# Moving the maximum's products ahead of the first weighing in each turn of an attention kernel on one core

## The chip, the cores and the metric

The kernel runs on one core of one Trainium2 chip. The core has TensorE (PE in the profile, with its weight loads listed apart as PEld), VectorE (DVE), ScalarE (ACT), GpSimd (POOL) and SyncE (SP). Each runs its own stream of instructions in order and waits for the others by semaphores. The metric is the device time of one execution in microseconds (us).

## What is computed

For each of 4 images (512 channels, 48 x 48 = 2304 positions) the layer is group norm, then attention with 8 heads of 64 channels over all 2304 positions, a 1x1 convolution beside it, and the residual. Cut to what matters:

```
h   = groupnorm(x)
q, k, v = (Wq @ h), (Wk @ h), (Wv @ h)          # per head: 64 x 2304
attn = softmax(q^T k)                           # per head: 2304 x 2304
out  = attn @ v
x    = x + gamma * out + Wsc @ h
```

## The kernel before

**Tiling.** Two heads are worked on together (a block; 4 images x 4 pairs = 16 blocks). Head 0 of the pair lies in rows 0 to 63 of TensorE, head 1 in rows 64 to 127, and products of the two halves come in pairs that run beside each other. A block has 6 chunks of 384 queries, so there are 96 chunks (n = 0 to 95). A chunk has 18 turns (k = 0 to 17), one for each 128 keys: 1728 turns, numbered s = 18 n + k.

**One turn on TensorE.** Precision is gained by splitting numbers into an upper and a lower part, so most things are done in several products.
- `score(n, k)`: six products of 384 columns (L477) into the tensor `SL`. It waits until ScalarE has read the scores of the turn before out of `SL` (semaphore `s_exp`).
- `top(U)`, U = s + 22: two products of 384 columns (L451) into `MX`, from which VectorE takes the largest score of each query (L794, one reduction for each `top`). This runs 22 turns ahead, since the maximum of a chunk must be known before its first score. There is one `MX`, so `top(U)` waits until the reduction of `top(U - 1)` has ended (semaphore `s_mxf`). The last 22 turns have no `top`.
- `weigh(s, part)`: the exponentials of turn s times the values, into `OB`. It has two parts, and each is six products of 129 columns (L516) and six of 65 columns (L513). The second part of turn s - 4 is done in turn s, and the first part of turn s - 3.
- `thirds(J, lo, hi)`: projections for the blocks to come (queries, keys, values, or the convolution), into `PJ`, cut into pieces of 128 columns that are spread over the turns: 9, 9, 5 and 13 pieces in turns 0 to 3, mostly 8 or 9 in the others. They are on L386 (384, 256 or 128 columns) or, for values, L384 (128 columns). In the last block (from chunk 90) nearly all of them are gone.

**The other engines.** ScalarE takes the exponential of `SL` into `PE32` (L634). GpSimd splits off its lower part `PLO` (L985). VectorE does the reductions (L794), and the parts of everything that leaves PSUM: L764, L772 and L758 for queries, values and keys, L780 for the convolution, L946 for the statistics of the next image.

**Change of chunk.** The sums of chunk n - 1 in `OB` are complete after `weigh(..., 1)` of its last turn, which stands in turn 2 of chunk n, between two parts of `thirds`. Then ScalarE copies `OB` out (L641, in its stream ahead of the exponential of turn 3), and VectorE adds the lower halves (L806, in its stream ahead of the reduction of turn 3). Only after L806 may `weigh` of the new chunk start in `OB` (semaphore `s_oe`, in turn 3). In turn 4 VectorE has two more pieces behind the reduction: L764 or L772, and the reciprocal L813.

In turn 3 `top` stands inside `thirds`, behind 7 of its 13 pieces. In turn 0 of six chunks a small product for the group norm's mean or variance (`root`, L426) also goes into `MX` behind the scores; VectorE takes it out (L829, L835), and `top` of this turn waits for that (`s_rtf`).

Of the kernel before, what the change touches and what calls it, by code (L numbers as in the profile page):

```python
# [38 lines left out]
TOPS = CHUNKS * MT  # L39
# [24 lines left out]
def block_of(k):  # L64

    b = max(i for i, at in enumerate(STARTS) if at <= k)
    lo = sum(THIRDS[STARTS[b]:k])
    return b, lo, lo + THIRDS[k]


def unit_in(J):

    if J < 0 or J >= 4 * CHUNKS:
        return None
    n, b = divmod(J, 4)
    if b == 2:
        return ("sc", n - 1) if n else None
    if n >= LAST:
        return ("sc", n) if J == 4 * (CHUNKS - 1) else None
    g, c = divmod(n, NCH)  # L80
    kind, part = AHEAD[3 * c + b - b // 3]
    return (kind, g + 1, part)
# [12 lines left out]
def root_unit(n, k):  # L95

    g, c = divmod(n, NCH)
    if k == MT - 1 and g % PAIRS == 1 and g // PAIRS + 1 < BATCH and c < 2:
        return ("r", g // PAIRS + 1, c)
    return None  # L100
# [18 lines left out]
def build(nc, x, wq, wk, wv, wsc, gamma, out):  # L119
    ctx = ExitStack()  # L120
    with ctx:
# [53 lines left out]
        def same_bank_before(u):  # L175
            i = PLACE[u]
            if i < 4:
                return None
            if i < OPENING:
                return UNITS[i - 4]  # L180
            return {PLACE[x] % 2: x for x in UNITS[OPENING - 4:OPENING] if PLACE[x] % 4 > 1}[(i - OPENING) % 2] \
                if i < OPENING + 2 else UNITS[i - 2]
# [152 lines left out]
        def _(pe):  # L335
# [3 lines left out]
            def left(u):  # L339
                if u[0] != "k":  # L340
                    pe.wait_ge(s_pjd, LEFT[u])
                elif u[1]:
                    pe.wait_ge(s_df, KCOUNT[u])
                else:
                    pe.wait_ge(s_kh, KCOUNT[u])
# [28 lines left out]
            def term(u, rows, i, a, end):  # L374

                kind, dst = u[0], bank(u)
                g, c = divmod(u[1], NCH) if kind == "sc" else u[1:]
                b, j = divmod(g, PAIRS)
                t, (wp, p) = i // 3, PARTS3[i % 3]
                edge = dict(start=rows.start == 0 and i == 0 and a == 0, skip_group_check=True,  # L380
                            stop=rows.start > 0 and i == TERMS - 1)
                if kind == "v":
                    m = c * QT + a
                    return pe.matmul(dst[:, a * P:(a + 1) * P], X[rows, b % 2, p, t, m * P:(m + 1) * P],  # L384
                                     WT[rows, 2, wp, t, j * P:(j + 1) * P], **edge)
                return pe.matmul(dst[:, a * P:end * P], WT[rows, WEIGHT[kind], wp, t, j * P:(j + 1) * P],  # L386
                                 X[rows, b % 2, p, t, c * CH + a * P:c * CH + end * P], **edge)

            def thirds(J, lo, hi):

                begun, ended = unit_in(J), unit_in(J - 1)
                if begun and lo == 0:
                    left(same_bank_before(begun))
                    if begun[0] == "k" and begun[1] % PAIRS == 0:
                        pe.wait_ge(s_gno, NCH * (begun[1] // PAIRS - 1) + begun[2] + 1)
                if ended and lo == 0:
                    pe.wait_ge(s_low, PLACE[ended] - OPENING + 1)
                for i in range(lo // 3, (hi + 2) // 3):
                    first, end = max(lo - 3 * i, 0), min(hi - 3 * i, 3)
                    for a in range(first, end):  # L400
                        last = i == TERMS - 1 and end == 3
                        if begun and (a == first or begun[0] == "v"):
                            one = term(begun, slice(0, D), i, a, end)
                            if last and (begun[0] != "v" or a == 2):
                                one.then_inc(s_low, 1)
                        if ended and (a == first or ended[0] == "v"):
                            one = term(ended, slice(D, P), i, a, end)
                            if last and (ended[0] != "v" or a == 2):
                                one.then_inc(s_pj, 1)
# [27 lines left out]
            def top(U):  # L437
                n, k = divmod(U, MT)
                g, c = divmod(n, NCH)
                i, t = divmod(k, KT)  # L440
                if k == 0:
                    pe.wait_ge(s_upper, UPPER["q", g, c])
                    pe.wait_ge(s_kh, KCOUNT["k", g, NCH - 1])
                if U:
                    pe.wait_ge(s_mxf, U)
                if U >= LEAD and root_unit(*divmod(U - LEAD - 1, MT)):
                    b, part = root_unit(*divmod(U - LEAD - 1, MT))[1:]
                    pe.wait_ge(s_rtf, 2 * b + part + 1)
                for h in range(2):
                    r = slice(h * D, (h + 1) * D)  # L450
                    last = pe.matmul(MX[:, h, 0:CH], QK[r, g % 2, QH, c * CH + i * P:c * CH + (i + 1) * P],  # L451
                                     QK[r, g % 2, KH, t * CH:(t + 1) * CH], start=True, stop=True)
                last.then_inc(s_mx, 1)

            def score(n, k):
                g, c = divmod(n, NCH)
                s = n * MT + k
                if s:
                    pe.wait_ge(s_exp, s)
                else:  # L460
                    for u in UNITS[OPENING - 4:OPENING]:
                        if PLACE[u] % 4 < 2:
                            left(u)
                if k == 0:
                    pe.wait_ge(s_cr, 16 * (n + 1))
                    pe.wait_ge(s_dk, KCOUNT["k", g, NCH - 1])
                q = slice(c * CH, (c + 1) * CH)
                keys = slice(k * P, (k + 1) * P)
                if k == 0:
                    for h in range(2):  # L470
                        r = slice(h * D, (h + 1) * D)
                        pe.matmul(SL[:, h, 0:CH], ones[r, :], CR[r, :, :], start=True, stop=False,
                                  skip_group_check=True)
                for a, b in ((DH, QH), (DL, QH), (DH, QL)):
                    for h in range(2):
                        r = slice(h * D, (h + 1) * D)
                        last = pe.matmul(SL[:, h, 0:CH], QK[r, g % 2, a, keys], QK[r, g % 2, b, q],  # L477
                                         start=False, stop=a == DH and b == QL, skip_group_check=True)
                last.then_inc(s_score, 1)
# [76 lines left out]
            for n in range(CHUNKS):  # L556
                for k in range(MT):
                    s = n * MT + k
                    U = s + LEAD
                    b, lo, hi = block_of(k)  # L560
                    score(n, k)
                    if k == 0 and n and root_unit(n - 1, MT - 1):
                        root(*root_unit(n - 1, MT - 1)[1:], U)
                    if k == LAG:
                        thirds(4 * n + b, lo, lo + 7)
                        if U < TOPS:
                            top(U)
                        thirds(4 * n + b, lo + 7, hi)
                        weigh(s - LAG, 0)
                        continue  # L570
                    if s > LAG:
                        weigh(s - LAG - 1, 1)
                    if k == LAG - 1 and n:
                        weigh(s - LAG, 0)
                    if U < TOPS:
                        top(U)
                    if lo == 0 and s > LAG:
                        weigh(s - LAG, 0)
                    if n and k in (11, 16):
                        result(n - 1, slice(0, D) if k == 11 else slice(D, P))  # L580
                    if k == LAG - 1:
                        thirds(4 * n + b, lo, lo + 3)
                        if n:
                            weigh(s - LAG, 1)
                        thirds(4 * n + b, lo + 3, hi)
                        continue
                    thirds(4 * n + b, lo, hi)
                    if lo and s > LAG:
                        weigh(s - LAG, 0)
# [500 lines left out]
```

## Time and profile before

| | |
|---|---|
| median of 3 runs | 2943.71 us (2942.43 to 2944.36) |
| the profiled execution's own time | 2940.95 us |
| its span in the profile | 2939.2 us |
| TensorE busy | 2891.7 us, 98% of the span |
| GpSimd, VectorE, ScalarE busy | 93%, 69%, 66% |
| granted TensorE clock, mean | 0.998 of full speed |

The span runs from the first to the last instruction in the profile; the execution's own time is 1.75 us longer. Busy shares are the time in which an engine has at least one instruction under way.

### The profile page before, as it was taken

What the parts mean: (1) busy time and instruction counts of PE and PEld (TensorE: products, weight loads), DVE (VectorE), ACT (ScalarE), POOL (GpSimd) and SP (SyncE); (2) the same over time, 40 slices, a digit from 0 to 9 for tenths busy, and PEclk for the clock granted to TensorE, in tenths of its full rate; (3) what the DMA queues carried; (4) which work ended last, traced back from release to release, by engine and by line L of the source; (5) the groups of instructions that cost most, each with busy time, mean ns of one, the idle gap of its engine ahead of it and who ended that gap; (6) DMA issues with size and microseconds to landing.
All of it is one profiled execution on the core that took longest, in us unless ns stands there. A gap on an engine that the chain in (4) does not pass through costs nothing. (4 is left out here: it accounts for less than half of the span.)

```text
span 2939.2 us, 153693 instructions
## 1 busy us (share of the span) xinstructions
PE 2891.7 (98%) x71226; PEld 2434.4 (83%) x71226; DVE 2016.3 (69%) x2665; ACT 1949.6 (66%) x3156; POOL 2741.2 (93%) x2043
## 2 busy tenths in 40 slices
PE   6999999999999999999999999999999999999999
PEld 4787888878888888888878888888888888888776
DVE  7777666666677666666677766666666666666663
ACT  4566676776666677677666667767666666666565
POOL 2799999999999999999999999999999999999998
PEclk9999999999999999999999999999999999999999
DMA  3011110110111011010011101101000000000000
GB/s 138 27 48 29 33 38 23 38 34 17 34 38 56 17 31 41 21 52 18 22 35 48 40 22 38 34 28 45 17 24 17 23 17 23 17 23 17 23 16 19
DMA packets 93090, 94.28 MB, mean 32 GB/s; under 512 B 44320, under 2 KB 90400, under 8 KB 92448
## 3 DMA queue, kind: packets, MB, share of 16 engines
q1 hardware_dynamic: 92448, 84.44, 9.5%
q8 instruction: 559, 9.16, 1.3%
q14 instruction: 83, 0.68, 0.1%
HBM read 56.10 MB, written 18.87 MB: 26 GB/s over the span
## 5 line engine op out<-in xcount | busy, mean ns | idle before, releaser
L985 POOL TENSOR_TENSOR PLO<-PE 128x768 f16<-128x768 f32 x1727 | 2502.8, 1471 | 136.3 <-ACT PE L634 110.3
L794 DVE TENSOR_REDUCE mx<-MX 128x2 f32<-128x768 f32 x1728 | 1657.3, 959 | 863.2 <-PE MX L451 844.2
L634 ACT ACTIVATE PE<-SL 128x768 f32<-128x768 f32 x1728 | 1402.2, 811 | 891.9 <-PE SL L477 882.5
L516 PE MATMUL OB<-V,PE 64*128 64x129 f16 x20736 | 1257.0, 218 | 0.8
L516 PEld LDWEIGHTS OB<-V,PE 64*128 64x128 bf16 x20736 | 1004.6, 94 | 219.7 <-DVE Oe L806 3.3
L477 PE MATMUL SL<-QK 64*128 64x384 f16 x10368 | 1167.5, 323 | 9.8 <-ACT PE L634 9.7
L513 PE MATMUL OB<-V,PLO 64*128 64x65 f16 x20736 | 984.5, 191 | 0.0
L386 PE MATMUL PJ<-X,WT 64*128 64x384 f16 (+2 forms) x7675 | 983.2, 301 | 0.0
L513 PEld LDWEIGHTS OB<-V,PLO 64*128 64x128 f16 x20736 | 741.1, 95 | 0.0
L451 PE MATMUL MX<-QK 64*128 64x384 f16 x3456 | 602.8, 323 | 7.7 <-DVE mx L794 6.1
L477 PEld LDWEIGHTS SL<-QK 64*128 64x128 f16 x10368 | 483.6, 94 | 124.2 <-ACT PE L634 15.9
L386 PEld LDWEIGHTS PJ<-X,WT 64*128 64x128 f16 x7675 | 453.5, 94 | 73.2 <-issue 0.7
L384 PE MATMUL PJ<-WT,X 64*128 64x128 f16 x6480 | 434.4, 216 | 0.0
L384 PEld LDWEIGHTS PJ<-WT,X 64*128 64x128 f16 x6480 | 354.5, 94 | 13.4
L451 PEld LDWEIGHTS MX<-QK 64*128 64x128 f16 x3456 | 208.1, 93 | 18.8 <-DVE mx L794 12.6
L650 ACT ACTIVATE attn<-Oe,rc 128x64 f32<-128x64 f32 x570 | 163.9, 337 | 0.0
L976 POOL TENSOR_TENSOR QK<-DF,QK 128x384 f16<-128x384 f32 x96 | 88.1, 918 | 3.8 <-ACT QK L601 3.8
L981 POOL TENSOR_TENSOR half<-attn,half 128x384 f16<-128x384 f32 x95 | 87.3, 919 | 0.0
L780 DVE SCALAR_TENSOR_TENSOR xr<-PJ,xr 128x384 f32<-128x384 f32 x96 | 52.6, 548 | 26.7 <-PE PJ L386 26.7
L641 ACT ACTIVATE Oe<-OB 128x390 f32<-128x390 f32 x96 | 47.8, 497 | 31.8 <-PE OB L513 31.8
L419 PEld LDWEIGHTS PJ<-identq,half 64*128 64x128 f16 x1140 | 57.4, 94 | 12.4
L1062 POOL TENSOR_TENSOR X<-gx,X 128x384 f16<-128x384 f32 x72 | 66.6, 925 | 0.0
(109 smaller groups left out, 986.2 us busy)
## 6 DMA issues: line engine op xcount, KB each, us to landing
gx<-x SPq DMA_DIRECT2D x36, 768.0 KB, 4.6
xr<-x SPq DMA_DIRECT2D x96, 192.0 KB, 2.4
out<-xr SPq DMA_DIRECT2D x96, 192.0 KB, 1.9
X<-x SPq DMA_DIRECT2D x6, 768.0 KB, 8.4
CR<-c SPq DMA_TRANSPOSE x96, 2.4
QK<-wk SPq DMA_DIRECT2D x1, 1024.0 KB, 9.0
QK<-wv SPq DMA_DIRECT2D x1, 1024.0 KB, 11.2
QK<-wq SPq DMA_DIRECT2D x1, 1024.0 KB, 11.9
```

Of the source, the lines that this page charges most:

```text
L384: return pe.matmul(dst[:, a * P:(a + 1) * P], X[rows, b % 2, p, t, m * P:(m + 1) * P], WT[rows, 2, wp, t, j * P:(j + 1) * P], **edge)
L386: return pe.matmul(dst[:, a * P:end * P], WT[rows, WEIGHT[kind], wp, t, j * P:(j + 1) * P], X[rows, b % 2, p, t, c * CH + a * P:c * CH + e ...
L451: last = pe.matmul(MX[:, h, 0:CH], QK[r, g % 2, QH, c * CH + i * P:c * CH + (i + 1) * P], QK[r, g % 2, KH, t * CH:(t + 1) * CH], start=Tru ...
L477: last = pe.matmul(SL[:, h, 0:CH], QK[r, g % 2, a, keys], QK[r, g % 2, b, q], start=False, stop=a == DH and b == QL, skip_group_check=True)
L513: last = pe.matmul(acc[:, 0:AW], PLO[r, s % PB, p0:p0 + P], v[:, 0:AW], start=False, stop=end, skip_group_check=True)
L516: last = pe.matmul(acc, upper, v, start=begin, stop=False, skip_group_check=True)
L634: act.activation(PE32[:, s % PB, :].rearrange("p (h n) -> p h n", h=2), SL[:, :, 0:CH], ACT.Exp, scale=1.0 / SS).then_inc(s_exp, 1)
L650: one = act.activation(attn[:, i * P + h * D:i * P + (h + 1) * D], Oe[:, h, i, 0:D], ACT.Copy, scale=rc[:, h, i, :])
L794: nc.vector.tensor_reduce(mx3[:, n % 2, :, k], MX[:, :, 0:CH], AX.X, ALU.max).then_inc(s_mxf, 1)
L976: nc.gpsimd.tensor_tensor(QK[:, g % 2, DL, c * CH:(c + 1) * CH], DF[:, KCOUNT[u] % 2, :], QK[:, g % 2, DH, c * CH:(c + 1) * CH], ALU.subtr ...
L981: nc.gpsimd.tensor_tensor(half[:, 1, :], attn[:, :], half[:, 0, :], ALU.subtract).then_inc(s_al, 1)
L985: nc.gpsimd.tensor_tensor(PLO[:, s % PB, :], PE32[:, s % PB, :], PE32[:, s % PB, :].bitcast(BF16)[:, 1:4 * CH:2], ALU.subtract).then_inc(s ...
```

## The change

Two things move in the stream of TensorE, and nothing else does; no instruction is added or removed. In each turn but the fourth (k = 3), `top(U)` moves from behind `weigh(s - 4, 1)` to directly behind the scores (and behind `root`, in the six turns that have one). In turn 2 it also moves ahead of `weigh(s - 3, 0)`. And in turn 2 the last `weigh` of the old chunk, which stood between 3 and 2 pieces of `thirds`, now stands behind all 5.

```
@@ -568,21 +568,20 @@
                         thirds(4 * n + b, lo + 7, hi)
                         weigh(s - LAG, 0)
                         continue
+                    if U < TOPS:
+                        top(U)
                     if s > LAG:
                         weigh(s - LAG - 1, 1)
                     if k == LAG - 1 and n:
                         weigh(s - LAG, 0)
-                    if U < TOPS:
-                        top(U)
                     if lo == 0 and s > LAG:
                         weigh(s - LAG, 0)
                     if n and k in (11, 16):
                         result(n - 1, slice(0, D) if k == 11 else slice(D, P))
                     if k == LAG - 1:
-                        thirds(4 * n + b, lo, lo + 3)
+                        thirds(4 * n + b, lo, hi)
                         if n:
                             weigh(s - LAG, 1)
-                        thirds(4 * n + b, lo + 3, hi)
                         continue
                     thirds(4 * n + b, lo, hi)
                     if lo and s > LAG:
```

TensorE's stream in turn 2 of chunk 48, from its scores to the scores of turn 3, before (L477 scores, L516 and L513 a part of `weigh`, L451 `top`, L386 `thirds`):

```order
L477 MATMUL SL<-QK 128x384 x6
L516 MATMUL OB<-V,PE 128x129 x6
L513 MATMUL OB<-V,PLO 128x65 x6
L516 MATMUL OB<-V,PE 128x129 x6
L513 MATMUL OB<-V,PLO 128x65 x6
L451 MATMUL MX<-QK 128x384 x2
L386 MATMUL PJ<-X,WT 128x384 x2
L516 MATMUL OB<-V,PE 128x129 x6
L513 MATMUL OB<-V,PLO 128x65 x6
L386 MATMUL PJ<-X,WT 128x256 x2
L477 MATMUL SL<-QK 128x384 x6
```

The same turn with the change:

```order
L477 MATMUL SL<-QK 128x384 x6
L451 MATMUL MX<-QK 128x384 x2
L516 MATMUL OB<-V,PE 128x129 x6
L513 MATMUL OB<-V,PLO 128x65 x6
L516 MATMUL OB<-V,PE 128x129 x6
L513 MATMUL OB<-V,PLO 128x65 x6
L386 MATMUL PJ<-X,WT 128x384 x2
L386 MATMUL PJ<-X,WT 128x256 x2
L516 MATMUL OB<-V,PE 128x129 x6
L513 MATMUL OB<-V,PLO 128x65 x6
L477 MATMUL SL<-QK 128x384 x6
```

`top` moved up past two parts of `weigh`, and the third part, which completes the old chunk, moved down past the 256 columns of `thirds`.

From `top` of turn 3 to behind `top` of turn 4 in the same chunk, before:

```order
L451 MATMUL MX<-QK 128x384 x2
L386 MATMUL PJ<-X,WT 128x384 x4
L516 MATMUL OB<-V,PE 128x129 x6
L513 MATMUL OB<-V,PLO 128x65 x6
L477 MATMUL SL<-QK 128x384 x6
L516 MATMUL OB<-V,PE 128x129 x6
L513 MATMUL OB<-V,PLO 128x65 x6
L451 MATMUL MX<-QK 128x384 x2
```

And with the change:

```order
L451 MATMUL MX<-QK 128x384 x2
L386 MATMUL PJ<-X,WT 128x384 x4
L516 MATMUL OB<-V,PE 128x129 x6
L513 MATMUL OB<-V,PLO 128x65 x6
L477 MATMUL SL<-QK 128x384 x6
L451 MATMUL MX<-QK 128x384 x2
L516 MATMUL OB<-V,PE 128x129 x6
L513 MATMUL OB<-V,PLO 128x65 x6
```

`top` of turn 3 stayed where it is, `top` of turn 4 moved up past one part of `weigh`: there is one part less between the two.

## Rows read from the trace of the kernel before

**Rows 1.** The page: busy time of each engine.

```profile
PE 2891.7 (98%) x71226; PEld 2434.4 (83%) x71226; DVE 2016.3 (69%) x2665; ACT 1949.6 (66%) x3156; POOL 2741.2 (93%) x2043
```

**Rows 2.** Waits of TensorE's weight loads, 100 to 2768 us: total, times, longest.

```profile
PEld SL L477 <- ACT PE L634: 4.0, 5, 1.2
...
PEld OB L516 <- DVE Oe L806: 1.5, 6, 0.3
...
PEld MX L451 <- DVE mx L794: 0.8, 3, 0.3
```

**Rows 3.** Timeline, turns 2 to 4 of chunk 48: start, duration, engine, line.

```profile
1517.09 0.33 PE L516 MATMUL OB<-V,PE 64*128 64x129 f16 x6
...
1517.35 0.33 PE L451 MATMUL MX<-QK 64*128 64x384 f16 x2
1517.51 0.33 PE L386 MATMUL PJ<-X,WT 64*128 64x384 f16 x2
1517.67 0.34 PE L516 MATMUL OB<-V,PE 64*128 64x129 f16 x6
1517.72 0.96 DVE L794 TENSOR_REDUCE mx<-MX 128x2 f32<-128x768 f32 x1 [0.50 <-PE MX L451]
...
1517.94 0.27 PE L386 MATMUL PJ<-X,WT 64*128 64x256 f16 x2
1518.05 0.65 PE L477 MATMUL SL<-QK 64*128 64x384 f16 x6
1518.14 0.50 ACT L641 ACTIVATE Oe<-OB 128x390 f32<-128x390 f32 x1 [0.30 <-PE OB L513]
1518.53 0.54 PE L386 MATMUL PJ<-X,WT 64*128 64x128 f16 x6
1518.67 0.56 DVE L806 TENSOR_TENSOR Oe<-OB,Oe 128x384 f32<-128x384 f32 x1
...
1518.91 0.32 PE L451 MATMUL MX<-QK 64*128 64x384 f16 x2
...
1519.28 0.96 DVE L794 TENSOR_REDUCE mx<-MX 128x2 f32<-128x768 f32 x1
1519.40 0.33 PE L516 MATMUL OB<-V,PE 64*128 64x129 f16 x6
...
1519.67 0.65 PE L477 MATMUL SL<-QK 64*128 64x384 f16 x6
1520.15 0.33 PE L516 MATMUL OB<-V,PE 64*128 64x129 f16 x6
1520.16 0.56 DVE L764 SCALAR_TENSOR_TENSOR QK<-PJ,QK 128x384 f16<-128x384 f32 x1
...
1520.42 0.32 PE L451 MATMUL MX<-QK 64*128 64x384 f16 x2
1520.58 0.33 PE L516 MATMUL OB<-V,PE 64*128 64x129 f16 x6
1520.63 0.18 DVE L813 RECIPROCAL rc<-Oe 128x6 f32<-128x6 f32 x1
```

**Rows 4.** Timeline, turns 3 and 4 of chunk 88.

```profile
2705.63 0.96 DVE L794 TENSOR_REDUCE mx<-MX 128x2 f32<-128x768 f32 x1
...
2705.97 0.32 PE L477 MATMUL SL<-QK 64*128 64x384 f16 x1
```

**Rows 5.** Timeline in the last block, where TensorE waits for the exponential.

```profile
2856.84 0.81 ACT L634 ACTIVATE PE<-SL 128x768 f32<-128x768 f32 x1 [0.29 <-PE SL L477]
...
2857.71 0.34 PE L477 MATMUL SL<-QK 64*128 64x384 f16 x2 [0.21 <-ACT PE L634]
```

**Rows 6.** Timeline, turns 8 and 9 of chunk 51 (values leave PSUM here).

```profile
1615.52 0.56 DVE L772 SCALAR_TENSOR_TENSOR V<-PJ,V 128x384 f16<-128x384 f32 x1
...
1616.59 0.36 PE L477 MATMUL SL<-QK 64*128 64x384 f16 x2
```

**Rows 7.** Timeline, turn 0 of a chunk with `root`.

```profile
295.52 0.16 DVE L829 COPY gn<-MX 128x4 f32<-128x4 f32 x1 [0.19 <-PE MX L426]
...
295.83 0.34 PE L451 MATMUL MX<-QK 64*128 64x384 f16 x2
```

More of the change, by code:

```diff
@@ L570, in _ @@
                         continue
+                    if U < TOPS:
+                        top(U)
                     if s > LAG:
@@ L574, in _ @@
                         weigh(s - LAG, 0)
-                    if U < TOPS:
-                        top(U)
                     if lo == 0 and s > LAG:
@@ L581, in _ @@
                     if k == LAG - 1:
-                        thirds(4 * n + b, lo, lo + 3)
+                        thirds(4 * n + b, lo, hi)
                         if n:
                             weigh(s - LAG, 1)
-                        thirds(4 * n + b, lo + 3, hi)
                         continue
```

## The prediction

> **What bounds the kernel now.** I read the page's busy times first. TensorE is busy 98% of the span [rows 1], so a step that moves within its stream can gain only what TensorE waits today, and each new wait costs its full length. Then the waits of its weight loads, since the load in front of a product is what a semaphore holds. Over 2668 us of steady work they come to 4.0, 1.5 and 0.8 us [rows 2], and the one on `top`'s reduction, which this change bears on, is the smallest. So there is nearly nothing to gain. The question is whether the new places make a wait, and the timeline of the one irregular spot, turns 2 to 4 of a chunk, answers it [rows 3].
>
> **The products themselves.** They are the same, in another order. One part of `weigh` takes 0.26 or 0.27 us to what follows it, whatever that is: 1517.09 to 1517.35 ahead of `top`, 1517.67 to 1517.94 ahead of `thirds`, 1519.40 to 1519.67 ahead of scores, all in [rows 3]. `top` takes 0.16 ahead of `thirds` and 0.16 ahead of `weigh` (1517.35 to 1517.51, 1520.42 to 1520.58), and the scores take 0.48 ahead of either (1518.05 to 1518.53, 1519.67 to 1520.15) [rows 3]. Only scores ahead of `top` are not shown; they are the same width, so I take 0.48. So the reordering costs nothing in itself. These differences are good to about 0.01, and a systematic 0.005 in each of 1,600 turns would be 8 us either way; I keep that for the range.
>
> **The ordinary turn.** `top` waits for the reduction of the `top` before it. That loop is, from [rows 3]: the products end 0.32 after their start, 0.05 more until VectorE begins (1518.91 + 0.32 = 1519.23, reduction at 1519.28), 0.96 for the reduction, and the release. The release I read where TensorE really waits: the exponential ends at 2856.84 + 0.81 = 2857.65, and the waiting product starts at 2857.71, 0.06 later [rows 5]. Sum 0.32 + 0.05 + 0.96 + 0.06 = 1.39 us. A turn is 1.62 (1518.05 to 1519.67) [rows 3]. `top` moves by the same 0.26 in all ordinary turns, so the distance between two stays a turn, and nothing waits. Cost 0.
>
> **Turn 3 to turn 4, the term that counts.** `top` of turn 3 keeps its place, 0.86 behind the start of its scores (1518.05 to 1518.91), while that of turn 4 moves from 0.75 to 0.48 behind its own (1519.67 to 1520.42 before). The distance of the two shrinks from 1.51 to 1.24 us, and the loop needs 1.39 [rows 3]. Step by step for chunk 48: the reduction of turn 3 starts at 1519.28 and ends at 1520.24; with the release `top` of turn 4 can start at 1520.30. It is wanted at 1519.67 + 0.48 = 1520.15. That is 0.15 us of waiting, in TensorE's own stream, with `weigh` and `thirds` queued behind it.
>
> The reduction may also begin a little later. The part of `weigh` that completes the old chunk now stands behind the last 256 columns of `thirds`, 0.11 us (1517.94 to 1518.05), so ScalarE's copy starts at 1518.25 in place of 1518.14 and VectorE's L806 at 1518.78 in place of 1518.67. VectorE takes its next work 0.47 us after the start of a 0.56 one (L764 at 1520.16, L813 at 1520.63) at the earliest, which gives 1519.25, no delay; if it waited for the end it would be 1519.34, a delay of 0.06 [rows 3]. I take 0.02. `weigh` of the new chunk, which needs L806's end (1518.78 + 0.56 + 0.06 = 1519.40), is wanted at 1519.40 and is not late; if it were, by a few hundredths, `top` of turn 4 would wait that much less, since the reduction sets its start anyway.
>
> The Trainium skill (VectorE: DVE Perf Modes, The DRAIN you can't avoid) says that after each VectorE instruction the pipeline empties before the next one begins. By that rule L806 would hold the reduction until 1519.34, 0.04 later than I take, and the sum would be 3.6 us higher. This trace does not agree for the pair L764 and L813, where the second starts 0.09 us before the first has ended; the pair L806 and L794 under pressure it does not show.
>
> In chunk 88 the same difference is larger: 2705.63 + 0.96 + 0.06 = 2706.65 against 2705.97 + 0.48 = 2706.45, so 0.20 [rows 4]. I worked it out for all 90 chunks in which TensorE is full (0 to 89), two of which stand in [rows 3, 4]: it lies between 0.09 and 0.21, with a mean of 0.17. With the 0.02 it is 0.19, times 90 = **17.1 us**.
>
> **Is it given back?** In turn 5 `top` is wanted at 1520.58 + 0.27 + 0.48 + 0.48 = 1521.81, plus the 0.17 lost (a part of `weigh`, nine pieces, the scores). The reduction of turn 4 starts behind L813 at the latest at 1520.63 + 0.18 = 1520.81 and is released at 1521.83 [rows 3]. No second wait, and no gain either: the turns after it are full, so the 0.19 stays lost. In the last block TensorE waits 0.21 us per turn for the exponential anyway [rows 5]; a wait for the maximum there hides behind that. Cost 0.
>
> **Other places.** In turn 2 `weigh` of the old chunk waits for the part ahead of it to end. Between them lie now 0.16 + 0.11 = 0.27 us of `thirds`; before it was `top` and 384 columns, 0.32. A pair of products ends about 0.16 after the next has begun (0.32 of duration against 0.16 to the next), and the release takes 0.06, so 0.22 is enough [rows 3, 5]. Cost 0; I allow 0.03 per chunk for the range. In the turns with `root`, `top` now follows `root` directly and waits until VectorE has taken its result: 295.52 + 0.16 + 0.06 = 295.74, while one part of `weigh` that used to fill this time comes behind [rows 7]. The loss is about 0.2, in three turns; in the three others TensorE is held soon after by the exponential. **0.6 us.**
>
> **Sum.** 17.1 + 0.6 = 17.7 us. On the profiled execution's own time, 2940.95, it gives 2958.7; the median of the runs is 2.8 above that execution, so I forecast 2943.7 + 17.7 = **2961 us**.
>
> **Rivals.**
>
> *Slower by more: two further waits in each chunk.* Work that leaves PSUM in turns 7 and 12 reaches VectorE in turns 8 and 13, ahead of the reduction. Now the reduction is wanted 0.27 earlier. In chunk 51 L772 starts at 1615.52. If the reduction may start 0.47 later, as L813 does, at 1615.99, it is released at 1617.01; `top` of turn 9 is wanted at 1616.59 + 0.48 = 1617.07 [rows 6]. That fits. If it starts only when L772 has ended, and the 0.05 more that it takes behind TensorE's products, at 1616.13, `top` waits 0.08. With 0.08 in turn 9 and half of that in turn 14, 90 times, it adds 11 us, and the same habit of VectorE adds 3.6 behind L806: 2961 + 14 = 2975. It decides once the start lies more than 0.53 behind that of L772. The section of the Trainium skill named above speaks for this case. Against it stands the early start of L813. Chance 0.14.
>
> *No change.* `top` of turn 4 waits as computed but the time is found again: the delay shortens the small waits in [rows 2], 6.3 us in all, and VectorE's reduction starts a little sooner than 0.05 behind the products. Or the distance of scores to `top` is larger than 0.48 as two products of another shape follow. Each would have to take some 0.13 out of 0.19; nothing in the rows does. 2943 to 2949, chance 0.13.
>
> *Faster.* A part of `weigh` takes 0.26 to 0.27, and its own columns (three pairs of 129 and three of 65, beside the 0.16 that a pair of 384 takes) would need 0.24. The loads of weights are what a stream of short products lacks time for, and the 0.02 may be lost at its end. If wide products directly ahead of the loads save it, each turn gets 0.02 faster: 1,600 times, 32 us, against 17.7 lost, so 2929. It decides from 0.015 per turn. Against it: the 0.02 is there behind scores (1520.15 to 1520.42) and behind `thirds` (1517.67 to 1517.94) alike [rows 3], and the change puts as many parts behind wide products as before. Chance 0.06.
>
> The forecast itself has 0.67.
>
> **The range.** Within the forecast: 0.13 to 0.23 us per chunk gives 12 to 21 us, and the order's 8 us either way widens that to about 2949 to 2971. To hold 8 in 10 with the rivals I take 2946 to 2975: the upper rival down to its full price, the no-change case in part. A measurement of this kernel tells 0.2% (5.9 us) from no change. Slower by more than that takes the forecast and the first rival, 0.80; within it 0.13; faster 0.07 with what the faster case leaves.
>
> **What would show it.** In the profile after, TensorE's wait on VectorE's L794 at `top` should go from 0.8 us to about 17 in some 90 pieces of 0.1 to 0.25, all in turn 4, the product starting 0.06 behind the reduction's end; the turn 3 reduction should start 1.2 to 1.3 us behind the scores as now. Waits at `top` in turns 9 and 14 would speak for the first rival; turn 4 without a wait would prove me wrong; ordinary turns that last other than 1.61 to 1.67 us would show that the order of the products does cost or gain.

## The result, and the profile after

| | before | changed |
|---|---|---|
| median | 2943.9 us (2942.43 to 2944.36, 4 runs) | 2956.3 us (2955.88 to 2958.39, 4 runs) |
| ratio, 95% interval | | 1.0048 (1.0036 to 1.006) |
| span of the profiled execution | 2939.2 us | 2954.1 us |

The kernel became slower by 12.4 us in the medians, with 10.6 to 17.7 us in the interval, and by 14.9 us between the two profiled spans (the execution profiled before, 2940.95 us, is faster than all four in the table, so this difference is somewhat larger than that of the medians). The forecast was 17.7 us.

The page after, busy times; TensorE is as full as in [rows 1]:

```profile
PE 2904.5 (98%) x71226; PEld 2325.2 (79%) x71226; DVE 1987.9 (67%) x2665; ACT 1947.0 (66%) x3156; POOL 2739.9 (93%) x2043
```

The waits of TensorE's weight loads after, 100 to 2780 us (total, times, longest), which answer to [rows 2]:

```profile
PEld MX L451 <- DVE mx L793: 33.9, 93, 0.5
PEld MX L451 <- issue: 7.6, 36, 0.5
PEld OB L516 <- DVE Oe L805: 6.6, 30, 0.2
PEld SL L477 <- ACT PE L633: 2.7, 3, 0.9
```

The wait of `top` (L451) for the reduction (now L793) went from 3 times to 93, and 90 of these, 32.3 us, lie in turn 4, one in each of the chunks 1 to 90. The total is larger than the loss. Directly behind the scores the load of `top` runs 0.16 us ahead of its product where nothing holds it, and the loads pause for about 0.06 us in front of it even then; the list counts both in each of the 90 entries of 0.35 to 0.37 us. So what the wait costs is read from the products. The 36 entries without a releaser are 30 in turn 14 and 6 in turn 0 with `root`; in turn 14 `top` still starts 0.49 behind its scores, so those 30 cost nothing. The 30 of L516 are the first `weigh` of the new chunk, which waits for the addition (now L805).

The timeline after, turns 3 and 4 of chunk 48, answers to [rows 3] (start, duration, engine, line; lines of VectorE and ScalarE are one lower than before):

```profile
1525.72 0.65 PE L477 MATMUL SL<-QK 64*128 64x384 f16 x6
1525.92 0.50 ACT L640 ACTIVATE Oe<-OB 128x390 f32<-128x390 f32 x1 [0.41 <-PE OB L513]
...
1526.45 0.56 DVE L805 TENSOR_TENSOR Oe<-OB,Oe 128x384 f32<-128x384 f32 x1 [0.63 <-ACT Oe L640]
1526.59 0.32 PE L451 MATMUL MX<-QK 64*128 64x384 f16 x2
...
1526.95 0.96 DVE L793 TENSOR_REDUCE mx<-MX 128x2 f32<-128x768 f32 x1
1527.07 0.34 PE L516 MATMUL OB<-V,PE 64*128 64x129 f16 x6
...
1527.34 0.65 PE L477 MATMUL SL<-QK 64*128 64x384 f16 x6
...
1527.97 0.34 PE L451 MATMUL MX<-QK 64*128 64x384 f16 x2
...
1528.15 0.33 PE L516 MATMUL OB<-V,PE 64*128 64x129 f16 x6
```

The reduction of turn 3 starts at 1526.95, 1.23 behind the scores of its turn, exactly as before (1519.28 - 1518.05 in [rows 3]). It ends at 1527.91, and `top` of turn 4 starts 0.06 later, at 1527.97, 0.63 behind its scores. Where nothing holds it, it starts 0.49 behind them, as in turns 8 and 9 of chunk 51 further down. Chunk 48 loses 0.14 to 0.15 us here.

From the starts of the scores in both traces I took the mean length of each turn over chunks 2 to 89. All numbers are us; the last column is the sum of all 18 turns.

| kernel | turn 2 | turn 3 | turn 4 | turns 5 to 12 | chunk |
|---|---|---|---|---|---|
| before | 1.713 | 1.623 | 1.680 | 13.047 | 29.683 |
| changed | 1.714 | 1.647 | 1.824 | 13.026 | 29.835 |

Turn 4 grew by 0.144, turn 3 by 0.024. Turns 5 to 12 together became 0.021 shorter. Turns 0 and 1 together grew by 0.009, nearly all of it in three of the six chunks with `root` (7, 31 and 55), 0.27 in each. The chunk grew by 0.152, times 90 is 13.7 of the 14.9 us between the spans; the rest lies ahead of chunk 2 and in the last block.

### The profile page after: what moved, and what is told of

It reads as the page before. It is cut to its first block and busy times, and to the rows that moved or that the text cites. A ratio compares the mean times of both kernels' runs of the same rounds, so it can differ in the third digit from the quotient of the medians.

```text
span 2954.1 us, 153693 instructions
## 1 busy us (share of the span) xinstructions
PE 2904.5 (98%) x71226; PEld 2325.2 (79%) x71226; DVE 1987.9 (67%) x2665; ACT 1947.0 (66%) x3156; POOL 2739.9 (93%) x2043
## 5 line engine op out<-in xcount | busy, mean ns | idle before, releaser
L793 DVE TENSOR_REDUCE mx<-MX 128x2 f32<-128x768 f32 x1728 | 1651.8, 956 | 798.5 <-PE MX L451 798.1
L516 PE MATMUL OB<-V,PE 64*128 64x129 f16 x20736 | 1185.1, 218 | 2.7 <-DVE Oe L805 2.1
L477 PE MATMUL SL<-QK 64*128 64x384 f16 x10368 | 1147.1, 323 | 8.5 <-ACT PE L633 8.0
L516 PEld LDWEIGHTS OB<-V,PE 64*128 64x128 bf16 x20736 | 892.6, 94 | 241.5 <-DVE Oe L805 10.6
L386 PE MATMUL PJ<-X,WT 64*128 64x384 f16 (+2 forms) x7675 | 958.7, 301 | 0.0
L513 PE MATMUL OB<-V,PLO 64*128 64x65 f16 x20736 | 942.2, 191 | 0.0
L513 PEld LDWEIGHTS OB<-V,PLO 64*128 64x128 f16 x20736 | 698.6, 95 | 0.0
L451 PE MATMUL MX<-QK 64*128 64x384 f16 x3456 | 584.1, 324 | 9.1 <-DVE mx L793 5.4
L477 PEld LDWEIGHTS SL<-QK 64*128 64x128 f16 x10368 | 442.6, 94 | 141.7 <-ACT PE L633 14.4
L386 PEld LDWEIGHTS PJ<-X,WT 64*128 64x128 f16 x7675 | 360.8, 93 | 52.1 <-issue 0.3
L384 PEld LDWEIGHTS PJ<-WT,X 64*128 64x128 f16 x6480 | 316.7, 94 | 2.1
L451 PEld LDWEIGHTS MX<-QK 64*128 64x128 f16 x3456 | 191.2, 94 | 147.9 <-DVE mx L793 46.0
L805 DVE TENSOR_TENSOR Oe<-OB,Oe 128x384 f32<-128x384 f32 x96 | 53.7, 559 | 66.9 <-ACT Oe L640 66.9
L757 DVE SCALAR_TENSOR_TENSOR DF<-PJ,KF 128x384 f32<-128x384 f32 x90 | 50.2, 558 | 25.7 <-ACT KF L610 24.5
```

Source lines behind the costliest of these rows:

```text
L513: last = pe.matmul(acc[:, 0:AW], PLO[r, s % PB, p0:p0 + P], v[:, 0:AW], start=False, stop=end, skip_group_check=True)
L516: last = pe.matmul(acc, upper, v, start=begin, stop=False, skip_group_check=True)
L793: nc.vector.tensor_reduce(mx3[:, n % 2, :, k], MX[:, :, 0:CH], AX.X, ALU.max).then_inc(s_mxf, 1)
```

## The experiments

Ratios are to the kernel before in the same batch; its medians there were 2942.6, 2942.7 and 2942.5 us. Runs a to d were one batch, e to g the next, h and i the last. The mean turns are worked out from the traces as above.

| run | median us | ratio, 95% interval | turn 2 | turn 3 | turn 4 | chunk |
|---|---|---|---|---|---|---|
| a_turn4_back | 2943.8 | 1.0005 (0.9996 to 1.0014) | 1.714 | 1.649 | 1.684 | 29.700 |
| b_split_kept | 2964.6 | 1.0075 (1.0062 to 1.0088) | 1.805 | 1.621 | 1.831 | 29.917 |
| c_late_weigh_alone | 2943.0 | 1.0003 (0.9994 to 1.0012) | 1.711 | 1.652 | 1.682 | 29.696 |
| d_turn3_later | 2972.6 | 1.0102 (1.0089 to 1.0116) | 1.714 | 1.646 | 1.990 | 30.011 |
| e_turn3_earlier | 2951.9 | 1.0033 (1.0021 to 1.0045) | 1.714 | 1.647 | 1.778 | 29.791 |
| f_turn3_earlier_split | 2950.1 | 1.0026 (1.0015 to 1.0037) | 1.807 | 1.621 | 1.677 | 29.768 |
| g_turn4_back_split | 2950.7 | 1.0028 (1.0017 to 1.0038) | 1.806 | 1.621 | 1.670 | 29.762 |
| h_turn2_before_turn3_earlier | 2944.2 | 1.0006 (0.9997 to 1.0015) | 1.713 | 1.636 | 1.694 | 29.709 |
| i_turn2_before | 2955.8 | 1.0045 (1.0033 to 1.0058) | 1.712 | 1.620 | 1.853 | 29.844 |

**a: turn 4 alone goes back.**

```
-                    if U < TOPS:
+                    if U < TOPS and k != LAG + 1:
                         top(U)
                     if s > LAG:
                         weigh(s - LAG - 1, 1)
+                    if U < TOPS and k == LAG + 1:
+                        top(U)
```

> The changed kernel, but in turn 4 alone top stands behind the first weigh again, as before. Theory 1 (the loss is the wait of turn 4's top for turn 3's reduction, 0.15 us in each of 90 chunks): that wait goes, what is left is the 0.02 us that turn 3 grew by and 1 to 2 us at root, so 2945 to 2948 us, and TensorE waits for the reduction in no turn 4. Theory 2 (the new order of products costs something in every turn, or the wait is only the place where it shows): 1,500 turns still have the new order, so it stays at 2950 to 2956 us.

The median is 2943.8 us, slightly under the range of theory 1, and not to be told from the kernel before. Turn 4 is at 1.684 again. The timeline of this run, turn 4 of chunk 48:

```profile
1520.52 0.96 DVE L795 TENSOR_REDUCE mx<-MX 128x2 f32<-128x768 f32 x1
...
1520.91 0.65 PE L477 MATMUL SL<-QK 64*128 64x384 f16 x6
1521.40 0.34 PE L516 MATMUL OB<-V,PE 64*128 64x129 f16 x6
...
1521.66 0.33 PE L451 MATMUL MX<-QK 64*128 64x384 f16 x2
```

The reduction starts 1.24 behind the scores of its turn (at 1519.28), as before, and ends at 1521.48. Now one part of `weigh` fills the time until then, and `top` comes at 1521.66. 16 of the 18 turns still have the new order. So the new order itself costs nothing that can be measured (the interval is -1.2 to +4.1 us), and the place of `top` in one turn of 18 made the loss.

Turn 5 has become the narrow one: its `top` comes 1.42 us behind that of turn 4, where the loop needs 1.39. The list of waits has 83 entries there, 16.8 us, for loads of `top` that lost their lead, and yet turn 5 is no longer than before (1.670 against 1.671). The list alone would have shown a loss where there is none.

**d: a larger dose of the same cause.** In turn 3:

```
-                        thirds(4 * n + b, lo, lo + 7)
+                        thirds(4 * n + b, lo, lo + 10)
                         if U < TOPS:
                             top(U)
-                        thirds(4 * n + b, lo + 7, hi)
+                        thirds(4 * n + b, lo + 10, hi)
```

> The changed kernel, with top of turn 3 behind 10 of its 13 pieces of thirds in place of 7, so 0.16 us later (three pieces of 128 columns). Theory 1: turn 3's reduction starts 0.16 later and top of turn 4 waits 0.16 more, 90 times, 14 us: 2970 to 2971 us, with 0.31 us of waiting in turn 4. Rival (the loss is not this wait): no change from 2956 us.

It measured 2972.6 us, 1.6 us above the expectation. Turn 4 grew by another 0.166 us for a `top` of turn 3 that is 0.16 later. Its timeline:

```profile
1535.43 0.32 PE L451 MATMUL MX<-QK 64*128 64x384 f16 x2
...
1535.80 0.96 DVE L793 TENSOR_REDUCE mx<-MX 128x2 f32<-128x768 f32 x1
...
1536.02 0.65 PE L477 MATMUL SL<-QK 64*128 64x384 f16 x6
...
1536.81 0.34 PE L451 MATMUL MX<-QK 64*128 64x384 f16 x2
```

`top` of turn 4 starts 0.05 behind the reduction's end (1536.76), and 0.79 behind its scores.

**e: a smaller dose, which meets L806.** In turn 3:

```
-                        thirds(4 * n + b, lo, lo + 7)
+                        thirds(4 * n + b, lo, lo + 4)
                         if U < TOPS:
                             top(U)
-                        thirds(4 * n + b, lo + 7, hi)
+                        thirds(4 * n + b, lo + 4, hi)
```

> The changed kernel, with top of turn 3 behind 4 of its 13 pieces of thirds in place of 7, so 0.16 us earlier, and the last weigh of the old chunk still behind all pieces of turn 2. Its products then end 1.03 us after the scores of turn 3 began, but L806 stands ahead of the reduction in VectorE's stream and starts at about 0.73 to 0.76. If VectorE takes the next work 0.47 us after L806's start, the reduction begins at 1.20 to 1.23, 0.03 to 0.06 earlier than now: 2951 to 2954 us. If it waits until L806 has ended (1.32), it begins 0.06 later than now and the kernel is slower, 2961 us. If L806 does not bind at all, the whole 0.16 is gained: 2942 to 2944 us.

It measured 2951.9 us, the first case. The timeline, turn 3 of chunk 48 (its scores start at 1523.76):

```profile
1524.46 0.33 PE L451 MATMUL MX<-QK 64*128 64x384 f16 x2
1524.49 0.56 DVE L805 TENSOR_TENSOR Oe<-OB,Oe 128x384 f32<-128x384 f32 x1 [0.63 <-ACT Oe L640]
...
1524.97 0.95 DVE L793 TENSOR_REDUCE mx<-MX 128x2 f32<-128x768 f32 x1
```

The products end at 1524.79, so 1524.84 would have been possible, but the addition stands ahead of the reduction (L805 here, L806 before). The reduction starts 0.48 after it, while it still runs (until 1525.05). Of the 0.16 that `top` moved, turn 4 got back 0.046 (1.824 to 1.778).

**b: the first part of the change without the second.**

```
-                        thirds(4 * n + b, lo, hi)
+                        thirds(4 * n + b, lo, lo + 3)
                         if n:
                             weigh(s - LAG, 1)
+                        thirds(4 * n + b, lo + 3, hi)
```

> The changed kernel, but the last weigh of the old chunk stands between 3 and 2 pieces of thirds in turn 2 again, 0.11 us earlier. Theory 1: the start of turn 3's reduction is set by top of turn 3 and not by L806, so the wait of turn 4 takes back what turn 3 gains: turn 3 gets 0.02 us shorter, the wait in turn 4 0.02 longer, total 2955 to 2957 us. Rival (the late last weigh carries a share of the loss through ScalarE's copy and L806): 0.05 to 0.1 us less per chunk, 2947 to 2952 us.

Both theories missed: it measured 2964.6 us, 8 us slower than the changed kernel. Turn 3 got shorter as theory 1 has it (1.647 to 1.621). Turn 4 grew by 0.007 (1.824 to 1.831) and not by the 0.02 expected, because the reduction of turn 3 also started 0.019 earlier (1.244 behind the scores in place of 1.263). The earlier addition alone did not do that: it starts at 0.625 here and at 0.646 in i, whose reduction still starts at 1.267. What did is not shown. What grew is turn 2, from 1.714 to 1.805. The waits of this run's weight loads, one row:

```profile
PEld OB L516 <- PE OB L513: 4.6, 29, 0.2
```

Only 29 of the 90 chunks are in it, so the length of turn 2 tells more. The last `weigh` of the old chunk works with the two heads' halves swapped, and therefore waits (`s_half`) until the part ahead of it has ended. In the kernel before, `top` and 3 pieces lay between the two. With `top` at the front only 3 pieces are left.

**f: e with the split.** Both edits, of e and of b.

> As the run before (top of turn 3 behind 4 pieces), and the last weigh of the old chunk 0.11 us earlier, between 3 and 2 pieces of thirds. If L806 was what bound the reduction of turn 3 in that run, it now starts 0.11 earlier (about 0.65), the reduction at 1.12, and top of turn 4 waits 0.01 to 0.04 us: 2944 to 2948 us, about as fast as the kernel before with all tops but one ahead of the weighing. If something else bound it, the two runs are alike.

It measured 2950.1 us, a miss, for the reason seen in b: turn 2 lasts 1.807. What it was made for came out. The timeline, turns 2 to 4 of chunk 48:

```profile
1524.13 0.26 PE L513 MATMUL OB<-V,PLO 64*128 64x65 f16 x6
1524.22 0.33 PE L386 MATMUL PJ<-X,WT 64*128 64x384 f16 x2
1524.45 0.35 PE L516 MATMUL OB<-V,PE 64*128 64x129 f16 x6
...
1525.46 0.56 DVE L806 TENSOR_TENSOR Oe<-OB,Oe 128x384 f32<-128x384 f32 x1 [0.60 <-ACT Oe L641]
...
1525.54 0.33 PE L451 MATMUL MX<-QK 64*128 64x384 f16 x2
...
1525.93 0.95 DVE L794 TENSOR_REDUCE mx<-MX 128x2 f32<-128x768 f32 x1
...
1526.45 0.66 PE L477 MATMUL SL<-QK 64*128 64x384 f16 x6
1526.94 0.34 PE L451 MATMUL MX<-QK 64*128 64x384 f16 x2
```

The first three rows show the wait of b as it is: the part ahead ends at 1524.13 + 0.26 = 1524.39, and the next part starts 0.06 later, at 1524.45, 0.23 behind the start of the `thirds` between them, which alone take 0.16. These 0.07 are most of the 0.09 by which turn 2 grew; the last 0.01 to 0.02 are not accounted for. The last rows show a turn 4 without loss: the addition starts at 1525.46, the reduction at 1525.93, and `top` stands 0.49 behind its scores.

**g: a with the split.** Both edits, of a and of b.

> The changed kernel with both parts undone at the change of chunk: top of turn 4 behind the first weigh, and the last weigh of the old chunk between 3 and 2 pieces. Left of the change: top ahead of the weighing in 16 of 18 turns (turns 0 to 2 and 5 to 17). Theory 1: these cost nothing but 1 to 2 us at root, 2944 to 2946 us. If the new order of products costs 0.005 us or more in each turn, 2951 us or more; if it saves as much, 2937 us or less.

It measured 2950.7 us, again a miss by what the split costs: turn 2, at 1.806, loses 0.09 in each chunk, 8 us, of which turn 3 gives back 2 (1.621 in place of 1.649 in a). The other two possibilities fall too: they would show in the ordinary turns, and these are as before. Turn 4 is 1.670.

**c: the second part of the change alone.** The kernel before with

```
-                        thirds(4 * n + b, lo, lo + 3)
+                        thirds(4 * n + b, lo, hi)
                         if n:
                             weigh(s - LAG, 1)
-                        thirds(4 * n + b, lo + 3, hi)
```

> The kernel before, with only the second part of the change: the last weigh of the old chunk stands behind all five pieces of thirds; top stays behind the first weigh everywhere. Theory 1: the first weigh of the new chunk waits some 0.02 us for L806, and no top waits, so 2944 to 2947 us. Rival (the later copy is passed on in full, 0.11 us per chunk): 2952 to 2955 us.

It measured 2943.0 us, not to be told from the kernel before. Turn 3 grew by 0.029 from the wait of the new chunk's first `weigh` for the addition, which starts 0.11 later (0.757 behind the scores in place of 0.646, means over the same chunks), and turns 5 to 12 together got 0.022 shorter.

**h and i: turn 2 as before.** With a and e settled, two runs put `top` back between the parts of `weigh` in turn 2, with 3 and 2 pieces as before. i is the changed kernel with this alone; h also has the edit of e.

```
-                    if U < TOPS:
+                    if U < TOPS and k != LAG - 1:
                         top(U)
                     if s > LAG:
                         weigh(s - LAG - 1, 1)
                     if k == LAG - 1 and n:
                         weigh(s - LAG, 0)
+                    if U < TOPS and k == LAG - 1:
+                        top(U)
```

> Turn 2 as in the kernel before (two parts of weigh, top, 3 pieces, the last weigh of the old chunk, 2 pieces), top of turn 3 behind 4 pieces in place of 7, top directly behind the scores in all other turns, turn 4 too. Theory 1 with its addition (the last weigh waits for the end of the part ahead of it, which needs more than 3 pieces between the two): turn 2 lasts 1.71 us again in place of 1.81, L806 starts at 0.65, the reduction of turn 3 at 1.12 to 1.16, and top of turn 4 waits 0.00 to 0.04 us. Total 1 to 4 us above the kernel before: 2944 to 2947 us. If the extra 7 us of the runs with the split were not that wait, turn 2 stays at 1.81 and the time at 2950 us.

> The changed kernel with turn 2 alone as in the kernel before. Theory 1: nothing in turn 2 bears on the wait of turn 4, whose reduction still starts behind top of turn 3 at 1.26: turn 4 lasts 1.82, turn 2 1.71, total as the changed kernel, 2954 to 2957 us. If the 7 to 8 us of the split are not the wait between the two parts of weigh, 2962 us or more.

Both came as expected: h 2944.2 us, i 2955.8 us. Turn 2 is at 1.71 in both, so the 0.09 of the split came from how little lay between the two parts. i loses as the changed kernel does: its turns 3 and 4 last 3.473 us together, those of the changed kernel 3.471. In h, `top` stands directly behind the scores in 16 of 18 turns, turn 4 among them, and the loss is gone because turn 3's `top` moved 0.16 up and the addition, 0.11 earlier than in e, was hardly in its way. The timeline of h, turns 3 and 4 of chunk 48:

```profile
1520.19 0.65 PE L477 MATMUL SL<-QK 64*128 64x384 f16 x6
...
1520.82 0.56 DVE L808 TENSOR_TENSOR Oe<-OB,Oe 128x384 f32<-128x384 f32 x1
...
1520.90 0.32 PE L451 MATMUL MX<-QK 64*128 64x384 f16 x2
...
1521.30 0.95 DVE L796 TENSOR_REDUCE mx<-MX 128x2 f32<-128x768 f32 x1
...
1522.30 0.34 PE L451 MATMUL MX<-QK 64*128 64x384 f16 x2
```

1.11 from the scores to the reduction in place of 1.23, and `top` of turn 4 is 0.49 behind its scores (1521.81), just in time. The addition still holds the reduction a little: it starts 0.48 behind L808, where the end of the products (1521.22) would have let it start at 1521.27. No version beat the kernel before.

## Why the prediction was right, point by point

**What bounds the kernel.** Right. TensorE had no waits to give back, and no order of `top` gained anything: a, c and h end within 0.1% of the kernel before.

**The products themselves.** Right. Scores ahead of `top`, which the rows of before did not show, take 0.487 us for the 0.48 assumed. In a, 16 of 18 turns have the new order and the time is that of before. Ordinary turns kept their length to 0.01 us.

**Turn 3 to turn 4.** Right in place, mechanism and nearly in size. Forecast was 0.17 us of waiting plus 0.02 for a later reduction. (By its own terms the mean over the 90 chunks comes out as 0.18, from 0.10 to 0.22; with the 0.487 it is 0.17.) Turns 3 and 4 together grew by 0.168; the 0.02 did not come. The mean start of the reduction is 1.263 us behind the scores against 1.266 before, although the addition starts 0.107 later (0.753 against 0.646). Run d adds to the wait what `top` of turn 3 is delayed, run e takes away what the addition lets it, run a removes it. The wait for the addition, which I had called not late, does cost 0.024 in turn 3, and `top` of turn 4 waits that much less, as the prediction said it would. In all 90 chunks `top` of turn 4 starts 0.06 behind the reduction's end, as forecast. The sign in the list of waits was mis-sized: 17 us in pieces of 0.1 to 0.25 were forecast and 33.9 stand there, for the reason given above.

**Given back.** Here the prediction missed a small term: "the turns after it are full, so the 0.19 stays lost". Turns 5 to 12 together are 0.021 us shorter, 1.9 us in 90 chunks. In chunks that project values the two halves of TensorE drift apart before the change: the scores of chunk 88 start as one product and then the other ([rows 4] shows x1 where [rows 3] has x6). So do those of turn 8 of chunk 51 before:

```profile
1614.96 0.32 PE L477 MATMUL SL<-QK 64*128 64x384 f16 x1
...
1615.02 0.65 PE L477 MATMUL SL<-QK 64*128 64x384 f16 x5
```

Behind a wait that holds both halves they start level. After the change, turns 8 and 9 of chunk 51:

```profile
1623.38 0.65 PE L477 MATMUL SL<-QK 64*128 64x384 f16 x6
1623.87 0.33 PE L451 MATMUL MX<-QK 64*128 64x384 f16 x2
1623.88 0.56 DVE L771 SCALAR_TENSOR_TENSOR V<-PJ,V 128x384 f16<-128x384 f32 x1 [0.36 <-ACT V L620]
...
1624.35 0.95 DVE L793 TENSOR_REDUCE mx<-MX 128x2 f32<-128x768 f32 x1
...
1625.00 0.65 PE L477 MATMUL SL<-QK 64*128 64x384 f16 x6
1625.49 0.33 PE L451 MATMUL MX<-QK 64*128 64x384 f16 x2
```

The same 0.02 appears in a and c, which have a wait in turn 3 and none in turn 4, so it does not hang on `top`'s place. Turns 6 to 12 are shorter by 0.019 to 0.022 in all nine runs. Most of it lies in two of a block's six chunks, the fourth and the fifth, which project values in these turns (51 and 88 are such): 0.04 to 0.06 in each. There the first products of the two halves start 0.06 us apart in turns 5 to 8 before, and under 0.02 in every run. But the second and third chunk, which drift by 0.05 to 0.06 before and become level too, gain only about 0.01. So levelling goes with the gain, and that it is the cause is not shown. In b, f, g, h and i turn 5 of the fifth chunk is 0.04 to 0.07 longer than before, for a reason that stays open, and so their turns 5 to 12 together are shorter by only 0.005 to 0.013.

**Turns with `root`.** Forecast 0.2 us in three chunks, 0.6 us. Three chunks lost 0.27 each, 0.8 us; the other three lost nothing.

**Turn 2.** The prediction said 0.22 us must lie between two parts of `weigh`, and that 0.27 do. Both held (f shows 0.23), and turn 2 kept its 1.71. What I did not draw from it was that the second part of the change is needed for the first: without it 0.16 lie there, and turn 2 lost 0.09 us in each chunk of b, f and g, 8 us, which three of my expectations missed.

**The rivals.** *Slower by more* falls. In the rows above the reduction starts 0.47 after L771, which still runs until 1624.44, and is released at 1625.36; `top` of turn 9 was wanted at 1625.49, where it starts. In the mean of 88 chunks `top` of turns 9 and 14 starts 0.49 us behind its scores, as in the turns beside them, so neither waits. Run e shows the same early start behind the addition. The Trainium skill (VectorE: DVE Perf Modes, The DRAIN you can't avoid) says that the next op does not start until the pipe is empty, and this is what the prediction took from it. The same section ends its first paragraph with an exception that the prediction left out: a next op that is not held starts earlier. The runs agree with the exception for these pairs: the reduction starts 0.08 to 0.09 us ahead of the end of L771, L805 and L808. *No change* falls on a: the loss is there and has one cause. *Faster* falls on the ordinary turns, which saved nothing.

**The sum.** 17.7 forecast. By the means it is 0.168 for turns 3 and 4, less 0.021 in turns 5 to 12, times 90, 13.2 us; with 0.8 at `root` 14.0, of the 14.9 between the spans. So the forecast was some 4 us too high: 2 us for the later reduction that did not come, and 2 for what turns 5 to 12 gave back. By the medians, 12.4 us, it stands at the upper end of the interval.

## What to carry to other kernels

When an instruction waits for another engine's answer to its own last turn, look at the distance between two of them in the irregular turns, and compare it with the loop there and back. Here the shift cost next to nothing where the neighbour moved along, and made nearly the whole loss in the one turn whose neighbour had not. Before filling work is taken away between two dependent parts, add up what is left between them: `top` was the filling between two halves of `weigh`, and only the second part of the change replaced it.

## What the runs showed that I had not expected

- Behind the waits at the change of chunk later turns got shorter: 0.02 us over turns 6 to 12 in the mean, in every run, and 0.04 to 0.06 in the two chunks of six that project values there.
- VectorE began its reduction before the end of the piece ahead of it, 0.47 to 0.48 us after that piece's start, also where the reduction was already due (runs e and h).
- The total of a weight load's waits overstates the loss: 33.9 us in the list against 15 us in the length of turns 3 and 4, and in a 16.8 us in turn 5 for no loss at all.
